# Turning attention's probabilities: from TensorE transposes to sixteen transfers and a VectorE transpose, with a new order of all engines' steps

## The reference, cut to what matters

```python
q, k, v = x @ Wq, x @ Wk, x @ Wv              # 8 heads of 64, in segments of 128 rows
for each segment:                             # a scan over the segments
    att_mem = (elu(q) + 1) @ mem / ((elu(q) + 1) @ z)
    sk  = elu(k) + 1
    mem = mem + sk.T @ v ;  z = z + sum(sk)
    att = softmax(q @ k.T / 8) @ v            # probabilities P, 128 x 128 for each head
    out = sigmoid(betas) * att_mem + (1 - sigmoid(betas)) * att
x = layernorm(x + out @ Wo)
W1, W2 = ternary(W1), ternary(W2)             # round(W / (mean|W| + eps)), clipped to -1..1
x = layernorm(x + relu(x @ W1.T + b1) @ W2.T + b2)
```

## Time and profile before

| what | value |
|---|---|
| time, median of 3 runs | 1925.68 us (1924.85 to 1925.83) |
| profiled execution: its own time / its span | 1925.02 us / 1923.0 us |
| TensorE busy | 1855.8 us, 97% |
| VectorE busy | 1330.2 us, 69% |
| ScalarE busy | 1244.2 us, 65% |
| GpSimd busy | 832.1 us, 43% |
| mean granted clock of TensorE | 0.994 of full |
| DMA | 117.50 MB, mean 61 GB/s |

### The profile page before, as it was taken

How to read it: one execution, slowest core, us unless ns; L and a number is a source line. 1 busy time by engine, 2 the same in 40 slices (tenths; PEclk the granted TensorE clock), 3 DMA queues, 4 the chain that set the end, 5 groups by cost and what they waited for, 6 DMA issues and landing times.

```text
span 1923.0 us, 44942 instructions
## 1 busy us (share of the span) xinstructions
PE 1855.8 (97%) x16575; PEld 1301.5 (68%) x16575; DVE 1330.2 (69%) x2603; ACT 1244.2 (65%) x2872; POOL 832.1 (43%) x964
## 2 busy tenths in 40 slices
PE   4689999999999999999999999999999999999998
PEld 3466777766777766677766677766677776667765
DVE  7786766676776777666767677677677677666652
ACT  5776666666676666666666666666667666666663
POOL 2113454443454443445444345444345444345442
PEclk9899999999999999999999999999999999999999
DMA  7513233223333233233322323322233322233110
GB/s 253 120 24 60 57 62 68 47 56 58 58 60 65 48 57 61 54 60 63 63 44 60 58 59 60 69 45 56 55 60 61 67 49 54 55 59 62 31 23 22
DMA packets 556423, 117.50 MB, mean 61 GB/s; under 512 B 529824, under 2 KB 533808, under 8 KB 555696
## 3 DMA queue, kind: packets, MB, share of 16 engines
q1 hardware_dynamic: 556208, 114.64, 29.5%
HBM read 50.54 MB, written 16.80 MB: 35 GB/s over the span
## 4 chain that ended last, share of the span: by engine, by line
PE 85%; DVE 8%; ACT 2%; SPq 2%; issue 1%; DMA 1%; DVEq 0%; POOL 0%; POOLq 0%; ACTq 0%
PE bank L437 10%; PE bank L438 10%; PE bank L453 10%; PE bank L454 9%; PE bank L287 6%; PE bank L288 6%; PE bank L289 6%; PE bank L375 3%; PE bank L418 3%; PE bank L420 3%; PE bank L419 3%; PE bank L301 3%; PE bank L302 2%; PE bank L303 2%; PE bank L354 2%; SPq L1543 2%
## 5 line engine op out<-in xcount | busy, mean ns | idle before, releaser
L437 PE MATMUL bank<-yt,w1t 128*128 128x256 f16 x2048 | 456.2, 273 | 1.7 <-ACT arena L1199 1.7
L438 PE MATMUL bank<-yt,w1t 128*128 128x256 f16 x2048 | 455.8, 273 | 0.0
L453 PE MATMUL bank<-w2t,arena 128*128 128x512 f16 x1024 | 388.8, 380 | 0.0
L454 PE MATMUL bank<-w2t,arena 128*128 128x512 f16 x1024 | 388.6, 379 | 0.0
L1196 ACT ACTIVATE arena<-bank,b_scaled,wscalars 128x256 f32<-128x256 f32 x512 | 276.9, 572 | 140.6 <-PE bank L438 140.6
L1138 ACT ACTIVATE prob<-bank,exp_bias,gscalars 128x128 f32<-128x128 f32 x512 | 227.4, 470 | 21.2 <-DVE exp_bias L736 21.1
L437 PEld LDWEIGHTS bank<-yt,w1t 128*128 128x128 f16 x2048 | 199.8, 98 | 34.8 <-ACT arena L1199 3.1
L438 PEld LDWEIGHTS bank<-yt,w1t 128*128 128x128 f16 x2048 | 200.3, 98 | 29.2
L1149 ACT ACTIVATE pt_hi<-bank 128x512 f16<-128x512 f32 x128 | 76.1, 596 | 205.8 <-PE bank L354 205.5
L1422 POOL TENSOR_TENSOR arena<-arena 128x512 f16<-128x512 f32 x128 | 146.8, 1157 | 143.7 <-ACT arena L1199 143.7
L1360 POOL TENSOR_SCALAR var_eps<-mean_var 128x1 f32<-128x1 f32 x64 | 20.0, 313 | 415.0 <-DVE mean_var L845 415.0
(11 more groups left out here) (192 smaller groups left out, 4766.6 us busy)
## 6 DMA issues: line engine op xcount, KB each, us to landing
rows<-in_L_attn_x SPq DMA_DIRECT2D x32, 512.0 KB, 3.6
out_rows<-rows SPq DMA_DIRECT2D x64, 256.0 KB, 2.3
x_blocks<-in_L_attn_x SPq DMA_DIRECT2D x248, 64.0 KB, 2.9
sk<-sk_t SPq DMA_DIRECT2D x480, 32.0 KB, 2.0
att_dot<-att_mem SPq DMA_DIRECT2D x480, 32.0 KB, 2.0
y_blocks<-rows SPq DMA_DIRECT2D x480, 32.0 KB
arena<-in_L_ffn_W SPq DMA_DIRECT2D x6, 1024.0 KB, 6.6
w2t<-in_L_ffn_W SPq DMA_DIRECT2D x2, 1024.0 KB, 13.2
```

The source lines that it names most:

```text
L437: pe.matmul(ps[:, c], w1t[:, k, cols], yt[:, g % 2, :, k], start=k == 0, stop=False)
L438: ins = pe.matmul(ps[:, c], w1t[:, k, cols], yt[:, g % 2, :, KT + k], start=False, stop=k == KT - 1)
L453: pe.matmul(banks[own][:], h_hi[:, f, toks], w2t[:, f, :], start=f == 0, stop=False)
L454: ins = pe.matmul(banks[own][:], h_lo[:, f, toks], w2t[:, f, :], start=False, stop=f == FT - 1)
```

## The change

P is no longer turned by TensorE. `prob` is laid out by blocks of 32 columns, SP moves 16 blocks with plain two-dimensional transfers (32 partitions of 2 KB in one piece each), and VectorE turns the whole of a group with one stream transpose of 2048 elements per partition. ScalarE and VectorE then split from SBUF instead of PSUM. `pt_hi` and `pt_lo` lie on `prob`'s memory. The exponentials of a group now wait for the whole product of the group before. TensorE's four `take`s for P are gone, so the rotation of the banks has 20 takes a turn instead of 24.

```diff
-        prob = sb("prob", [P, TG, H, P])
-        pt_hi = sb("pt_hi", [P, TG, H, P], F16)
-        pt_lo = sb("pt_lo", [P, TG, H, P], F16)
+        prob = sb("prob", [P, 4, TG, H, 32])
+        p_blocks = sb("p_blocks", [P, 4, TG, H * 32])
+        p_halves = prob[:].rearrange("p a t h n -> p (a t h n)").bitcast(F16).rearrange("p (q t h c) -> p q t h c", q=2, t=TG, h=H)
+        pt_hi, pt_lo = p_halves[:, 0], p_halves[:, 1]
...
-            def turn_p(g, t, half):                       # TensorE
-                b = take(("p", g, t, half))
-                pe.wait_ge(sem["pexp"], by_half(g, t, half))
-                for i in range(4):
-                    ins = pe.transpose(ps[:, i], prob[:, t, 4 * half + i], ident32[:])
...
+            def turn_p(g):                                # VectorE
+                flat_p = p_blocks[:].rearrange("p b t f -> p (b t f)")
+                dve.wait_ge(sem["pblocks"], MOVED * (g + 1))
+                dve.transpose(flat_p, flat_p).then_inc(sem["pturn"], 1)
+            def p_split(g, t):                            # VectorE
+                dve.wait_ge(sem["pt_hi"], by_t(g, t))
+                for b in range(4):
+                    cols = slice(32 * b, 32 * b + 32)
+                    ins = dve.scalar_tensor_tensor(out=pt_lo[:, t, :, cols], in0=p_blocks[:, b, t].rearrange("p (h n) -> p h n", h=H),
+                                                   scalar=2.0 ** 13, in1=pt_hi[:, t, :, cols], op0=ALU.mult, op1=ALU.subtract)
...
             def exponentials(g, t, half):                 # ScalarE
                 if g:
-                    act.wait_ge(sem["pturn"], by_half(g - 1, t, half))
+                    act.wait_ge(sem["pv"], by_t(g - 1, 1))
...
+            def p_split(g, t):                            # ScalarE
+                act.wait_ge(sem["pturn"], g + 1)
+                act.activation(pt_hi[:, t].rearrange("p h (b n) -> p h b n", b=4), p_blocks[:, :, t].rearrange("p b (h n) -> p h b n", h=H),
+                               ACT.Copy, scale=2.0 ** 13).then_inc(sem["pt_hi"], 1)
...
+            def move_p(g):                                # SP
+                sp.wait_ge(sem["pexp"], by_half(g, 1, 1))
+                if g:
+                    sp.wait_ge(sem["pt"], by_t(g - 1, 1))
+                for b in range(4):
+                    for a in range(4):
+                        sp.dma_start(p_blocks[32 * a:32 * a + 32, b].rearrange("p t f -> p (t f)"),
+                                     prob[32 * b:32 * b + 32, a].rearrange("p t h n -> p (t h n)")).then_inc(sem["pblocks"], 16)
```

More of the change, by code:

```diff
@@ L511, in _ @@
             spread_max(0)
-            for g in range(NG + 2):
+            for g in range(NG + 3):
+                ffn_up(g - 3, 2)
+                if g == 2:
+                    for n in range(8, 12):
+                        turn_w(n)
+                project_qk(g - 1, "q", 1)
+                if g == 1:
+                    turn_bias_max()
+                ffn_up(g - 3, 3)
+                if g == 1:
+                    spread_bias_max()
+                ffn_up(g - 3, 4)
                 if g == 0:
@@ L514, in _ @@
                     turn_max(1)
-                if g == 1:
-                    for n in range(8, 12):
+                if g == 2:
+                    for n in range(12, 16):
+                        turn_w(n)
+                scores(g - 1, 0)
+                turn_att(g - 2, 0)
+                read_memory(g - 1, 0)
+                ffn_up(g - 3, 5)
+                ffn_down(g - 3, 0, 0)
+                project_v(g - 1, 0)
+                turn_att(g - 2, 1)
+                if g == 2:
+                    for n in range(16, 20):
+                        turn_w(n)
@@ new lines, in _ @@
+                project_v(g - 1, 1)
+                scores(g - 1, 1)
+                ffn_up(g - 3, 6)
+                if g == 0:
+                    turn_bias()
+                project_out(g - 2, 0)
+                project_out(g - 2, 1)
+                ffn_up(g - 3, 7)
+                ffn_down(g - 3, 0, 1)
+                read_memory(g - 1, 1)
+                if g == 2:
+                    for n in range(20, 24):
+                        turn_w(n)
+                update_memory(g - 1, 0)
@@ L517, in _ @@
+                attend(g - 1, 1)
+                if g == 1:
+                    for n in range(0, 4):
                         turn_w(n)
                 ffn_up(g - 2, 0)
[L519 to L523, removed]
                 if g == 2:
@@ L541, in _ @@
[L541 to L555, removed]
@@ L571, in _ @@
[L571 to L585, removed]
@@ L1432, in _ @@
                 fill_memory(0, live)
-            for g in range(NG + 2):
+            for g in range(NG + 3):
+                inverse_std(g - 3, 0, 1)
+                yt_lo(g - 2, 0)
+                yt_lo(g - 2, 1)
+                gate_mix(g - 1, 0, False)
+                gate_mix(g - 1, 1, False)
+                add_bias(g - 2, 0)
+                if g == 1:
+                    scale_bias()
                 h_rest(g - 2, 1)
                 h_rest(g - 2, 3)
-                add_bias(g - 2, 0)
-                if (g + 1) % (LIVE * NSEG) < LIVE and LIVE * NSEG <= g + 1 < NG:
-                    fill_memory((g + 1) // (LIVE * NSEG), place(g + 1)[2])
                 at_lo(g - 1, 0)
```

407 lines of the change are left out of this document (191 added, 216 removed).

## The result

| | before | after |
|---|---|---|
| time, median of 4 runs each on one chip | 1925.76 us (1924.85 to 1926.86) | 1949.27 us (1946.72 to 1951.15) |
| profiled execution: its own time / its span | 1925.02 / 1923.0 | 1950.38 / 1948.6 |
| mean turn in the middle | 57.16 us | 57.43 us |
| first FFN matmul | 130.33 | 148.97 |

The ratio is 1.0121, 95% interval 1.0103 to 1.0139: slower by 23 us, where 47 us less was forecast. (In the experiments on sk's twelve and on SP's extra issues one of four executions lay a tenth above the others: the ratios leave it out, the medians in the table count it and are 1920.9 and 1943.2 without it.)

A forecast was written before the change was run, and what follows sets the result against it. TensorE's queue was taken to bound the steady turn, 57.1 - 1.9 = 55.2 us. First FFN matmul at 150 plus 1726 behind it gave 1876 span, so 1878 us; own range 1870 to 1887, whole range 1863 to 1908.

The forecast's parts named there:

- What bounds the kernel now: Steady stage: TensorE's queue is the clock, a turn of 57.11 us; in the opening TensorE waits for others.
- What is removed: TensorE: four jobs of turning P go, 1.9 us a turn, 57 us over 30 full turns.
- The steady turn of 55.2 us: Middle of the kernel: TensorE's turn of 57.1 us less 1.9 for turning P.
- What is added on VectorE and ScalarE: Transpose 2.4 us, eight differences 2.7 to 3.5; VectorE gets 2.4 to 3.2 more a turn, ScalarE no change; costs nothing.
- Rival (d): VectorE's eight differences collide with GpSimd, 4 us late, 2 us of each turn: 1925 to 1940 us; chance 0.04.
- The 78 to 80% for VectorE: VectorE's forecast busy share of the shorter turn, with 2.4 to 3.2 us added on 41.9 of 60.
- What is added on SP: SP's queue: sixteen transfers a turn at 0.4 us, 6.4 us; SP at 47 to 48 of 55, not the bound.
- Does the turned P come in time?: Steady turn: P complete at 25 to 27 us, the waits covered, with slacks of 3, 2 and 1 us.
- The opening: Before the first FFN matmul: it moves from 130.33 to 150, giving back 14 us; 1726 us remain behind it.
- the W2 part: Opening: last raw W2 load, issued behind P's first transfers, lands within 13.2 us and gives the threshold at 85.
- Rival (c): SP's ring of y, gates, attention, sk and P becomes the period: 1926 to 1950 us; chance 0.10.
- `45.1 + 16c`: SP's ring in us at price c per P issue; decides from 0.63, slower than before from 0.74.

The follow-up runs named there:

- sk's twelve: Changed kernel without the four diagonal ones of sk's sixteen transfers (left out of the computation): 1922.26 us, ratio 0.9943 to the kernel before.
- SP's extra issues: Kernel before, with sixteen small idle transfers a turn added on SP in its queue's gap: 1946.34 us, ratio 1.0068.

## Why the prediction was wrong, by its steps

- **What bounds the kernel now**, and that leaving TensorE's queue is a gain as long as nobody comes late: right. With one issue for P the kernel runs at 1868.
- **What is removed** (1.9 us a turn): right in size, 1.4 by doubling the turns, 2.0 by taking them out together with the new order. The steady turn of 55.2 us is there in every version whose rings are short enough: 54.94 to 55.34.
- **What is added on VectorE and ScalarE**: right. Transpose, differences and ScalarE's copy (mean ns behind the busy us):

```profile
L741 DVE SCALAR_TENSOR_TENSOR prob<-p_blocks,prob 128x256 f16<-128x256 f32 x256 | 90.1, 414 | 1.1 <-ACT prob L1143 1.1
L733 DVE STREAM_TRANSPOSE p_blocks<-p_blocks 128x2048 f32<-128x2048 f32 x32 | 74.0, 2312 | 137.8 <-DMA p_blocks<-prob 137.8
...
L1143 ACT ACTIVATE prob<-p_blocks 128x1024 f16<-128x1024 f32 x64 | 64.1, 1049 | 186.9 <-DVE p_blocks L733 186.9
```

  2.31 us against 2.4, and eight times 0.41 = 3.3 against 2.7 to 3.5. Rival (d) didn't happen. The 78 to 80% for VectorE are 77 to 78 if 41.9 of 60 is first put on a turn of 57.1; the trace has 43.91 of 60, 73%.
- **What is added on SP** ("I take 0.4"): this is the step that failed. It measured 0.66 in the mean of 29 turns (0.59 is the median of one issue; a few take up to 1.9). The only rows of the same shape, 32 partitions, were the strided series at 0.65 to 0.73, and they had it. I took the lower end from rows of 128 partitions. Such a row does take 0.33 or 0.60 by what is queued ahead, as `amax_dram` shows, but P's lone issue takes 0.56 behind an idle stretch too.
- **Does the turned P come in time?** P does, but y's issues behind P's ended too late. P was complete 28.8 us after the first FFN matmul, which is 25.2 into the turn, as forecast. From there 10.6 for P's issues, 11.3 for y's and 5.7 behind them make 52.8, and `ffn_up(0)` wants `yt` at 51.6: a turn of 56.4, the second ring. With 0.4 for each of P's issues it would have been 48.6.
- **The opening**: right in its time, 148.97 against 150, and in the threshold, 82.7 against 85. That is luck in part: the W2 part was issued 4 us later than I had put it (72.3), behind P's slower sixteen, but landed in under 6 us where I had allowed 13.2. Behind it lie 1948.6 - 149.0 = 1799.6 us against 1726 forecast. Of these 74 us the turn has 30 x (57.43 - 55.2) = 67.
- **Rival (c)** is what happened, but not by its sum, which makes the kernel slower than before only from 0.74. Its first part, 2 + 4 + 5.1 = 11.1 us from y's last issue to attention's first, measured 11.12, by luck in the parts: 5.5 until the split is done and 5.6 for the gates. Its `45.1 + 16c` gives 55.7 at 0.66, which is some 14 us over the forecast in 29 turns and still faster than before. The turn measured 57.46 in the mean of 27. The other 1.8 us: y's sixteen took 11.2 and not 10.4 (0.8), the small issues and the steps between series 1.6 and not 0.9 (0.7), attention's 11.2 and not 11.0 (0.2), sk's 11.3 and not 11.7 (-0.4), and SP's waits for the exponentials, where TensorE's ring is the longer, 0.4. So by this sum P's price alone costs a part of the gain; that the kernel became slower took the low prices of the other terms as well, above all y's. I had priced y by its cheapest row: in the kernel before its series takes 10.4 to 14.7 us. And it was one ring of two: that through TensorE's scores and the exponentials stood in no rival, though its steps are those of the paragraph on P's coming in time. It says what a repair must shorten first: P's or y's issues. Four of either brought 2.3 to 2.5 us a turn, four of sk's or attention's 0.6.

## What to carry to other kernels

Price a small transfer by its issue: for these of 32 partitions 0.66 us of the issuing engine at 64 bytes to 2 KB a partition, sixteen of them some 11 us. Take the mean of rows of the same shape rather than the best one, for every series in the queue and not only for the new one. Before adding issues to a queue, write down every ring that passes it, with the waits between, at the prices of a full queue; an edit that removes work from the busiest engine gains only until the longest ring is the turn, and beyond that costs. To repair, cut what lies in all the long rings, even with copies on an engine that has time.

## What was not expected of the hardware

- An issue of 32 partitions costs the same for 2 KB, 1 KB and 64 bytes a partition: means of 10.57, 10.55 and 10.66 us for sixteen, 0.66 to 0.67 each; on SP and on ScalarE (10.6) alike. Of the two prices of `amax_dram`, 0.33 behind a gap and 0.60 behind a series, P's issues show only one. One issue for 1 MB to DRAM took 0.33, and its way back 0.44 each for four. Why the one is cheaper than the sixteen the runs don't tell.
- TensorE's mean granted clock was 0.994 before, 0.981 after and 0.988 with one issue for P, nearly all of it lost in the opening: from 800 to 1200 us it was 1.00 in all three. With P issued by ScalarE, where TensorE waits 7.4 us in each turn, it was 0.929, and 0.95 in that stretch. From 60 to 120 us it was 0.80 after and 0.90 before, although the engine was busy about as long (43.5 and 44.2 us). No run changed that alone, so that what it cost the opening stays open.
